# Graph attention: shifts of the exponentials for two heads at once, and ScalarE two heads ahead

## The reference, cut to what matters

```
score = s_src + s_dst + <diff, a_dif> + <|diff|, a_abs> + <hr_src * hr_dst, a_prd>   # per head and edge
alpha = leaky_relu(score, negative_slope=0.2)
m = segment_max(alpha, src);  ex = exp(alpha - m[src])
att = ex / (segment_sum(ex, src)[src] + 1e-16)
out = segment_sum(att * h_e[dst], src)
```

## Time and profile before

| | us |
|---|---|
| median of 3 runs (2223.29 to 2227.28) | 2226.81 |
| the profiled execution | 2236.88 |
| its span | 2235.0 |
| PE busy (share 95%) | 2114.6 |
| DVE busy (47%) | 1049.3 |
| ACT busy (32%) | 720.5 |
| POOL busy (25%) | 554.9 |

### The profile page before, as it was taken

The page is one execution under the profiler, slowest core; times in us unless marked ns, Lnnn a source line. Parts: engine busy times, 40 slices in busy tenths (PEclk is TensorE's granted clock), DMA queues, the critical chain, the costliest instruction groups (busy, mean ns, idle before and its releaser), DMA issues.

```text
span 2235.0 us, 21978 instructions
## 1 busy us (share of the span) xinstructions
PE 2114.6 (95%) x8162; PEld 1280.8 (57%) x8162; DVE 1049.3 (47%) x2182; ACT 720.5 (32%) x1214; POOL 554.9 (25%) x467
## 2 busy tenths in 40 slices
PE   5899887799999999999999999999999999999998
PEld 3477554698666556544665565565565544444443
DVE  8897677788563333365454354345345200000002
ACT  1477655677331110022332342242251111111110
POOL 4577773443220100012012003003002200122202
PEclk9999999799999799999999999999999899999999
DMA  9522212731111102111011011011010677778732
GB/s 345 173 41 30 30 13 55 194 91 60 69 50 57 57 5 101 38 62 66 11 57 67 14 57 64 17 57 59 3 53 27 251 282 301 294 300 302 299 124 74
DMA packets 61508, 237.48 MB, mean 106 GB/s; under 512 B 23343, under 2 KB 28419, under 8 KB 39276
## 3 DMA queue, kind: packets, MB, share of 16 engines
q1 hardware_dynamic: 31898, 168.25, 21.0%
q0 software_dynamic: 26336, 62.19, 9.1%
q10 hardware_dynamic: 3168, 5.63, 0.7%
HBM read 204.06 MB, written 31.96 MB: 106 GB/s over the span
## 4 chain that ended last, share of the span: by engine, by line
PE 78%; DVE 11%; issue 4%; POOL 2%; DMA 2%; ACT 2%; PEldq 0%; PEld 0%; ACTq 0%; SPq 0%; DVEq 0%; POOLq 0%
PE PS L737 11%; PE PS L744 10%; PE PS L1038 10%; PE PS L1431 7%; PE PS L1440 7%; PE PS L1469 7%; PE PS L888 3%; PE PS L1076 2%; PE PS L1317 2%; PE PS L1234 2%; PE PS L1337 2%; PE PS L1338 2%; PE PS L755 1%; PE PS L1216 1%; DMA pair_scores<-TS,SIDX 1%
## 5 line engine op out<-in xcount | busy, mean ns | idle before, releaser
L2008 POOL TENSOR_TENSOR RSTD<-VE,HALF 125x1 f32<-125x1 f32 x100 | 81.1, 811 | 975.2 <-DVE VE L2178 975.2
L1038 PE MATMUL PS<-XT,WR 128*128 128x500 f32 (+2 forms) x992 | 233.6, 393 | 8.4 <-ACT XT L1537 3.5
L888 PE MATMUL PS<-HR,HOT 125*125 125x512 f32 x800 | 208.9, 408 | 18.2 <-DVE HOT L2322 18.2
L3036 DVE TENSOR_TENSOR AR<-AR,PS 128x512 f32<-128x512 f32 (+1 forms) x44 | 30.3, 688 | 405.5 <-PE PS L1440 405.5
L744 PE MATMUL PS<-WR,XT 128*125 128x512 f32 (+1 forms) x464 | 206.2, 592 | 0.6 <-DVE AR L2820 0.3
L1038 PEld LDWEIGHTS PS<-XT,WR 128*128 128x128 f32 x992 | 144.9, 193 | 87.7 <-issue 72.4
L888 PEld LDWEIGHTS PS<-HR,HOT 125*125 125x125 f32 x800 | 145.3, 189 | 59.2 <-DVE HOT L2322 19.2
L2026 POOL DMA_INDIRECT pair_sums<-CW,SIDX x80 | 135.6, 1696 | 54.2 <-DMA pair_sums<-CW,SIDX 22.1
L744 PEld LDWEIGHTS PS<-WR,XT 128*125 128x125 f32 x464 | 87.1, 193 | 89.4 <-issue 85.4
L737 PE MATMUL PS<-XT,WR 128*128 128x313 f32 (+3 forms) x432 | 124.7, 447 | 1.8 <-DVE CW L2286 1.3
L1967 ACT ACTIVATE AR<-PS 128x512 f32<-128x512 f32 (+1 forms) x44 | 26.3, 597 | 300.2 <-PE PS L1431 300.2
(11 more groups left out here) (435 smaller groups left out, 3926.5 us busy)
## 6 DMA issues: line engine op xcount, KB each, us to landing
WR<-in_qkv SPq DMA_DIRECT2D x12, 1024.0 KB
WR<-in_omm SPq DMA_DIRECT2D x12, 1024.0 KB
pair_scores<-CNT SPq DMA_DIRECT2D x1, 12212.0 KB, 35.7
AR<-pair_scores SPq DMA_DIRECT2D x5, 2187.5 KB
AR<-in_x_a SPq DMA_DIRECT2D x10, 1024.0 KB, 9.5
AR<-in_x_b SPq DMA_DIRECT2D x10, 1024.0 KB, 5.1
AR<-in_x_c SPq DMA_DIRECT2D x10, 1024.0 KB, 7.2
WR<-in_x_a SPq DMA_DIRECT2D x8, 1024.0 KB, 9.0
```

The lines of the kernel that those rows point to most:

```text
L888: last = mm(DIFF[m % 4], HOT[g % 2][0:P, k, tile(j)], HR[0:P, k, :, b, :], start=(k == 0 and b == 0), stop=(k == NT - 1 and b == 1))
L1038: last = mm(by_tile(s)[:, t0:t1, :], w[:, k, 128 * m:128 * (m + 1)], XT[:, k, P * t0:P * t1].rearrange("p (c n) -> p c n", n=P), start=(k ...
L2008: g.tensor_tensor(RSTD[:, t:t + 1], VE[:, t:t + 1], HALF[:, :], ALU.pow)\
```

## The change

On VectorE `shift(k)` becomes `shift_pair(k)`, which makes the shifts of heads k and k + 1 with the same three operations on two columns, and is called in every second turn. Its first operation is a scalar_tensor_tensor, since the added term is no longer one column per operation. On ScalarE both `bent` of a pair come ahead of both `exp_scores` of the pair.

```diff
             for k in range(4):
                 bent(k)
-                if k:
+                if k in (1, 3):
                     exp_scores(k - 1)
+                if k == 1:
+                    exp_scores(k)
             turned_counts(0)
             for k in range(HEADS_ALL):
+                if k % 2 and k + 4 < HEADS_ALL:
+                    bent(k + 4)
                 if k + 3 < HEADS_ALL:
                     exp_scores(k + 3)
-                if k + 4 < HEADS_ALL:
+                if k % 2 == 0 and k + 4 < HEADS_ALL:
                     bent(k + 4)
...
-            def shift(k):
+            def shift_pair(k):
+
                 t, h = divmod(k, HEADS0)
-                z = SH[:, t % 2, h, :]
-                dve.wait_ge(raw_taken, k + 1)
-                top = HM[:, t % 2, 0, h:h + 1]
-                v.tensor_scalar(z[:, 1:2], top, -0.8, UP[:, t, h:h + 1], ALU.mult, ALU.add)\
+                pair = slice(h, h + 2)
+                of_bent, of_score = SH[:, t % 2, pair, 1], SH[:, t % 2, pair, 0]
+                dve.wait_ge(raw_taken, k + 2)
+                top = HM[:, t % 2, 0, pair]
+                v.scalar_tensor_tensor(of_bent, top, -0.8, UP[:, t, pair], ALU.mult, ALU.add)\
                  .then_inc(vector_step, 1)
-                v.tensor_scalar(z[:, 0:1], top, -0.2, None, ALU.mult)
+                v.tensor_scalar(of_score, top, -0.2, None, ALU.mult)
                 dve.wait_ge(vector_step, n.add(vector_step))
-                v.tensor_scalar(z[:, 1:2], z[:, 1:2], 0.0, None, ALU.min).then_inc(negmax_ready, 1)
-                n.add(negmax_ready)
+                v.tensor_scalar(of_bent, of_bent, 0.0, None, ALU.min).then_inc(negmax_ready, 2)
+                n.add(negmax_ready, 2)
...
             for k in range(4):
                 raw_scores(k)
-                shift(k)
                 if k % 2:
+                    shift_pair(k - 1)
                     merge(1 + k // 2)
...
-                if k + 4 < NT * HEADS0:
-                    shift(k + 4)
+                if k % 2 and k + 4 < NT * HEADS0:
+                    shift_pair(k + 3)
```

## The result

| | before | changed |
|---|---|---|
| median of 5 runs each, same chip | 2227.28 (2223.29 to 2232.99) | 2244.42 (2238.08 to 2245.99) |
| ratio, 95% interval | | 1.0065 [1.0043, 1.0087] |
| profiled execution, span, mean granted clock | 2236.88, 2235.0, 0.970 | 2244.42, 2242.6, 0.969 |

The account below looks back on a forecast made before the run. TensorE carries most of the chain; inside the first attention, VectorE's scores and count product, then TensorE's next scores. 0.18 + 0.92 + 3 x 1.35 + 3 x 0.30 + 1.96 = 8.0 us on 2226.8 gives 2234.8, range 2224 to 2244.

Parts of the forecast that it names:

- Step 1: VectorE: twenty shifts of 0.30 us go, 6 us; only nine on the chain, 2.7 us if nothing else becomes last.
- Rival A: VectorE's gain reaches the end: -2.7 us, 2224.1, or 2220.8 with all 20 shifts; chance 0.10.
- Step 2: ScalarE's count copy comes 1.23 us later, so TensorE's L956 is 1.2 us late once in eight heads.
- Rival D: The PSUM slot did not hold L956, so its delay is nothing: 3.6 us in all, 2230.4; chance 0.12.
- Step 3: ScalarE's late high half of LEFT delays VectorE's L2465: +1.35 us per stretch with counts, +0.30 without.
- Step 4: Beginning: heads 0 to 3 keep their times, then exp(4) costs +0.18 us; first stretch with counts +0.92.
- Step 5: End: the last pair is shifted where head 39 was, so TensorE turns head 39 1.96 us later.
- rival B: TensorE's clock falls behind wider gaps in three or four more stretches, 3.1 us each: 2244 to 2247; chance 0.17.
- Rival C: The 1.80 us gap before the turn 8 stretch shrinks, clock holds, 3.1 us come back: 2231.7; chance 0.13.

Follow-up runs that it names:

- e2: Kernel before with single shifts kept but ScalarE's new order, both bent of a pair ahead of its exponentials: 2237.98 us, ratio 1.0032.
- e3: Changed kernel with ScalarE's copy of the turned counts moved to the top of its turn: 2244.13 us, ratio 1.0061 to before.
- e6: Changed kernel with single shifts and ScalarE's old order for heads 0 to 3 and 36 to 39 only: 2238.62 us, ratio 1.0042 to before.
- e4: As e3, with ScalarE's copy of the high half of LEFT also first in its turn: 2236.19 us, ratio 1.0018 to before.
- e8: e5 with pairs up to the end, so single shifts for heads 0 to 3 only: 2234.03 us, ratio 1.0008 to before.
- e5: e4 with single shifts and ScalarE's old order for heads 0 to 3 and 36 to 39: 2229.23 us, ratio 0.9994 to before.
- e1: Changed kernel with pairs kept but ScalarE's old order, exp(k + 3) ahead of bent(k + 4), in every turn: 2271.40 us, ratio 1.0207 to before.
- e7: Changed kernel run again with no edit: 2245.46 us, ratio 1.0071 to before.
- e0: Kernel before run again with no edit: 2231.68 us, ratio 1.0016 to before.

## Why the prediction was right and wrong

The sign, the mechanism and the places were right; 8.0 us was too small. Medians differ by 17.1, the ratios (1.0065, 1.0071) say 14 to 16. To separate work from clock I laid a line through 75 runs of the kernel before: each 0.01 of mean granted clock less goes with 15.8 us more. At one clock (0.972) before takes 2230.4 us and the changed kernel 2239.4 (11 runs), +9.0; the rest, some 5 us, goes with its lower mean clock. That is an estimate from a line, not a measurement of its own; by the same line e2 is at 2235.9, e3 at 2236.1, e6 at 2237.1, e4 at 2230.4, e8 at 2229.3, e5 at 2227.4 and e1 at 2252.5 (its clocks lie below all that the line was laid through). e8 is thus 1.9 us above e5, which is the late tail without its clock.

- *Step 1, VectorE's gain doesn't arrive:* right. It is worth 0.3 us a stretch only where ScalarE's copies come early (e4). Rival A is out. In the steady part a pair takes 0.33 or 0.34 us from its start to that of the next operation, where 0.30 was taken with bounds of 0.30 and 0.40; at the start it cost 1.9, by a wait that is read in the last section.
- *Step 2, L956 behind the count copy:* right. It was said 1.2 us late; the trace shows 1.02 us idle ahead of it in turns 4, 12 and 20, and the copy started 1.19 us later in its turn; in turn 28 TensorE was itself late. e3 gave back 1.28 us in a stretch with counts. Rival D is out.
- *Step 3, LEFT's high half:* right. 14.2 and 12.43 were said, 14.27 and 12.48 measured, and e4 takes it away. Of 3 x 1.35 there were 1.40, 1.40 and 1.75; of 3 x 0.30 two were 0.35 and 0.38, and the third lay in turns 7 to 11, where the clock of before hides it.
- *Step 4, the beginning:* wrong, the mis-sized term: 0.18 was forecast and 1.99 us measured in the first two traces, of which 1.3 are in every trace with pairs there. I took heads 0 to 3 to keep their times because each has another head's room. The last operation of their second pair is blocked by GpSimd's merge for 1.65 us, and the exponential behind it comes 1.25 us late. "Bounds 0.30 to 0.40" was read from rows of the steady part alone, where no merge is near. The 0.92 of the first stretch with counts, too, was a little too small and does not quite follow from its terms (0.18 + 1.2 - 0.30, less the 0.18 already counted, is 0.90); it came out as 1.23.
- *Step 5, the end:* the work was right (1.96 said, 1.84 in e2 at full clock), the price was not. In the changed kernel the tail is 4.77 us longer and 2.6 more are lost behind it.

The end in the changed kernel: GpSimd, and TensorE behind it, as forecast; then the clock.

```profile
542.24 1.30 POOL L2062 TENSOR_TENSOR AR<-AR,MASK 125x625 f32<-125x625 f32 x1 [2.77 <-ACT MASK L1709]
543.50 1.27 POOL L2067 TENSOR_TENSOR X<-X,Y 125x512 f32<-125x512 f32 x1
544.72 1.29 POOL L2062 TENSOR_TENSOR AR<-AR,MASK 125x625 f32<-125x625 f32 x1
```
```profile
543.59 0.81 PE L984 MATMUL PS<-CS,AR 125*125 125x125 f32 x5 [1.36 <-POOL AR L2062]
...
546.07 1.41 PE L984 MATMUL PS<-CS,AR 125*125 125x125 f32 x5 [0.46 <-POOL AR L2062]
```
```profile
547.00:550.00 3.00, 3.00 (x17) 3.00 (x15) 2.03 (x5) 0.00 (x0) 0.00 (x0) 0.50 0.14 47
```

The five transposes that took 0.81 us take 1.41 at the lower level (0.50 is 1.2 GHz). The granted clock of the tail is 0.77 to 0.83 in all six traces with pairs to the end (changed, e7, e1, e3, e4, e8), and 0.76 in e6; it is 1.00 in before, e0, e2 and e5.

So rival B was the missing part as far as these traces tell, in another place than I had put it: I had expected it in the middle, at 3.1 us each, where it came in the stretches with counts of e7 and in the last one of the changed kernel (14.61), at 0.35 us each. The cost was at the end, where a gap of 1.36 us and another stand ahead of work that nothing else covers. That this holds for most executions rests on one or two traces of each kernel and on the lower mean clock of the runs. Rival C, the clock that holds in turns 7 to 11, came in both traces of the changed kernel (idle 1.55 us ahead instead of 1.80), and e0, unchanged, had 1.66 us of that gain.

What sets the fall stays open, and it isn't the length of the idle time ahead alone. e6 fell behind a gap of 1.21 us, e5 did not behind 1.23:

```profile
541.56 0.78 PE L985 MATMUL PS<-CS,AR 125*125 125x125 f32 x5 [1.21 <-DVE AR L2522]
```
```profile
525.74 0.78 PE L985 MATMUL PS<-CS,AR 125*125 125x125 f32 x5 [1.23 <-DVE AR L2522]
```

In turn 8 the clock fell behind the same 1.55 us in e4, e5 and e6 and held in changed, e3, e7 and e8; and in e2 it held behind the longest gap of that place, where before had fallen behind 1.80:

```profile
440.84 0.38 PE L972 MATMUL PS<-HRT_HIGH,LEFT 128*125 128x314 f32 x1 [2.20 <-DVE HM L2479]
```
```profile
438.83:450.95 12.12, 10.11 (x85) 10.09 (x86) 10.68 (x28) 9.18 (x13) 5.28 (x4) 1.00 0.11 18
```

So the forecast's reading of 1.80 against 1.08 us as the difference between a fall and none, in rival B, doesn't hold.

## What to carry to other kernels

Saving instructions on a shared engine by making one wait for two results also makes the first result wait for the second; follow what is queued behind that result in strict order, above all copies that empty a PSUM slot, and move these ahead of the wait before counting the saving. A new idle time of TensorE can have two prices, its length and the clock behind it, and the second is paid where nothing covers the work that follows. A duration read in the steady part doesn't hold for a prologue where another engine does other work beside it.

## What the hardware showed that was not expected

*A third of a microsecond that became two.* VectorE and GpSimd in the changed kernel at the end of the prologue:

```profile
413.52 0.15 DVE L2493 TENSOR_SCALAR SH<-HM 125x2 f32<-125x2 f32 x1
413.70 1.65 DVE L2495 TENSOR_SCALAR SH<-SH 125x2 f32<-125x2 f32 x1
415.27 0.80 DVE L2389 TENSOR_TENSOR CNT<-AR 125x625 f32<-125x625 f32 x1
```
```profile
413.53 1.80 POOL L2072 TENSOR_TENSOR G<-AR 125x625 f32<-125x625 f32 x1
```

The last operation of the pair ends at 415.35, GpSimd's merge at 415.33. The same pair of rows stands in e1, e3, e4 and e7 (1.65 or 1.66 us). The one-column form beside the same merge took 0.15 us; in e2, with single shifts, the merge had even started 0.12 us earlier:

```profile
408.56 0.15 DVE L2493 TENSOR_SCALAR SH<-SH 125x1 f32<-125x1 f32 x1
408.63 2.28 DVE L2389 TENSOR_TENSOR CNT<-AR 125x625 f32<-125x625 f32 x1
```
```profile
408.44 1.80 POOL L2072 TENSOR_TENSOR G<-AR 125x625 f32<-125x625 f32 x1
```

There VectorE's own merge, a tensor_tensor, is what waits (2.28 us instead of 0.80), and it costs nothing: the first product with the counts comes at 14.19 us as before. The shift got through ahead of it.

The Trainium skill, "SBUF — State Buffer", section "SBUF: two separate sides", says that VectorE in some of its modes and GpSimd share a pair of ports as an exclusive lock: who starts first has it for its whole instruction, and the other is blocked. The trace agrees with the blocking, 1.65 us.

It isn't only that row. In the eleven traces a two-column operation of a pair started inside a GpSimd tensor_tensor, with more than 0.2 us of it left, 16 times: the last one five times, and the first one, which writes to another place, eleven times. Each ended 0.01 to 0.03 us behind GpSimd's, after up to 1.66 us. A one-column operation did so some 200 times and never took more than 0.22 us. The longest wait of a first operation is in e5 and e8:

```profile
425.82 0.94 DVE L2502 SCALAR_TENSOR_TENSOR SH<-HM,UP 125x2 f32<-125x2 f32 x1
```
```profile
425.20 1.54 POOL L2061 TENSOR_TENSOR AR<-AR,BENT_SPARE 125x625 f32<-125x625 f32 x1
```

So a pair also changes what each operation waits for, and its cost depends on what GpSimd does at that moment.

*The clock can fall behind idle times of 1.21 to 1.43 us* (e6, changed, e7), and it holds behind 1.55 (changed) and 2.20 us (e2). The spread of the kernel before over its runs (2219.8 to 2241.1) goes for a large part with the mean granted clock.
